# Expert stage of a gated cross-attention and mixture-of-experts block: one TensorE semaphore for each step of a pair, copies and picks in other steps, no clear behind the result scatters

## The chip, the cores and the metric

The kernel runs on one core of a Trainium2 chip. The metric is the device time of one execution in microseconds (us), the median of several runs; less is better. The core has five engines with queues of their own: TensorE (PE in the profile, its weight loads PEld), VectorE (DVE), ScalarE (ACT), GpSimd (POOL) and SyncE (SP). They meet by semaphores alone. Transfers are issued from SP, ACT and POOL and share 16 DMA engines.

## What is computed

The reference, cut to what matters here (x is 4 x 1024 tokens of 256 numbers):

```python
x = x + tanh(g_xattn) * xattn(layernorm(x), ctx_768, mask)
h = layernorm(x)                       # 4096 tokens x 256
topk_idx, topk_w = router(h)           # 6 of 32 experts a token
routed = sum over the token's 6 experts e of  w_e * (relu(h @ up_e.T) ** 2) @ down_e.T    # 256 -> 128 -> 256
shared = (relu(h @ up_s.T) ** 2) @ down_s.T                                               # 256 -> 512 -> 256
x = x + tanh(g_ffn) * (routed + shared)
```

All of it is float32. The 4096 x 6 routed rows are dealt with expert by expert, in tiles of 128 rows that belong to one expert.

## The kernel before

**Stages.** The first stage goes over the 32 token tiles: attention, router, and on POOL the scatter of each normed row to its six places in `routed_rows` in DRAM. The expert stage follows, and it is the one that changes. It has 224 tiles of 128 rows, taken two at a time: `N_PAIRS` = 112 pairs. A short tail adds the last results and stores them.

**A pair p on its way.** SP loads its two row tiles into `ring` (`mid` in the rows), six pairs deep (`load_rows`, L351). PE transposes them into PSUM (`rows_t`, L1337), ACT copies that to `xt` (`save_rows_t`, L581) and copies the two experts' up weights to `w_up` (`copy_up`, L594). PE multiplies (`expert_up`, L1349). DVE squares the positive part into `h_t` (`relu_square`, L977 and L979). PE multiplies with the down weights (`expert_down`, L1364). The result is scaled by the router's weight and goes to `y_sb`, one of eight buffers, by ACT for an even pair (L603) and by DVE for an odd one (L986); both are called `save_out`. POOL scatters `y_sb` to `token_parts` in DRAM, two indirect DMAs a pair (L442). Weights and destinations come from `pick_rows` on DVE (L963 to L972), once for two pairs; SP reloads a place of the ring only after it.

**Steps.** Each engine runs through the same steps p by a loop written out in its own order. On PE a step is `expert_up(p)`, `rows_t(p + 2)`, `expert_down(p - 1)`, and then in 20 steps (`SHARED_STEP`: p = 2, 7, 12 to 97) a piece of the shared expert (L1235 or L1244). PE signals three times in a step: `s_eup`, `s_xtp` and `s_edn`, each with the last matmul of its part. DVE starts on step p's hidden values at `s_eup`, ACT on the rows of pair p + 2 at `s_xtp`, and `save_out` at `s_edn`.

**Adding parts.** Once all pairs of a segment of tokens are scattered, ACT loads six parts of a token tile back (L616) and DVE adds them to `x_all` in three pieces, one a step (L994, L996 and L997, L999). `PART_LOAD` says in which steps. There are 28 such tiles, the first load in step 32; the last four tiles are loaded by SP at the end and summed on PE (L1390).

**The clear.** Behind every scatter POOL runs `pause`: it waits for the clear before, and clears 320 bf16 numbers of a buffer that nobody reads (L413).

```python
            def pause():
                if paused[0]:
                    pool.wait_ge(s_pause, paused[0])
                else:
                    pool.wait_ge(s_xb, NT)
                paused[0] += 1
                nc.gpsimd.memset(bias_o[:].bitcast(BF16)[:, 0:PAUSE], 0.0).then_inc(s_pause, 1)
```

Of the kernel before, what the change touches and what calls it, by code (L numbers as in the profile page):

```python
# [61 lines left out]
DONE = [-(-((TOPK * P * t + NE * (P - 1)) // P) // 2) for t in SEG_END[:-1]]  # L62
PART_LOAD = {DONE[g] + 4 + 3 * i: 4 * g + i for g in range(6) for i in range(4)}
PART_LOAD.update({DONE[6] + 4 + 2 * i: 24 + i for i in range(4)})
STORED = sum(p + 13 < N_PAIRS for p in PART_LOAD)
N_EARLY, N_LAST = len(PART_LOAD), NT - SEG_END[6]
SHARED_STEP = {2 + 5 * i: i for i in range(8 * (NBLK - GAP) - TB)}


def flamingo_block(nc, x, ctx_t, mask, g_xattn, g_ffn, w_q, w_k, w_v, w_o, b_o, gate_t, e_bias,  # L70
# [7 lines left out]
    with ExitStack() as ctx:  # L78
# [189 lines left out]
        s_ld = [sem(f"rows_loaded_{i}") for i in range(6)]  # L268
        s_xtp = sem("rows_t_psum")
        s_xts = sem("rows_t")  # L270
        s_eup = sem("expert_hidden_psum")
        s_ewu = sem("expert_up_weights_copied")
        s_eht = sem("expert_hidden_t")
        s_edn = sem("expert_out_psum")
        s_ey = [sem(f"expert_out_by_{e}") for e in ("act", "dve")]
# [34 lines left out]
        def _(sp):  # L310
# [32 lines left out]
            def load_rows(p):  # L343
                if p % 2 == 0:
                    sp.load(regs[p // 2 % 4], row_i[0:1, 2 * p:2 * p + 4])
                if p >= 6:
                    sp.wait_ge(s_xtp, p - 5)
                    sp.wait_ge(s_pick, (p - 6) // 2 + 1)
                for j in range(2):
                    at = sp.snap(regs[p // 2 % 4][p % 2 * 2 + j], min_val=0, max_val=DUMMY + NE * P)  # L350
                    sp.dma_start(ring[:, p % 6, j, :], rows[bass.ds(at, P), :]).then_inc(s_ld[p % 6], 16)  # L351
# [9 lines left out]

            sp.wait_ge(s_edn, N_PAIRS)
            for i in range(N_LAST):
# [11 lines left out]
        def _(pool):  # L375
# [63 lines left out]
            for p in range(N_PAIRS):  # L439
                pool.wait_ge(s_ey[p % 2], p // 2 + 1)  # L440
                for j in range(2):
                    nc.gpsimd.indirect_dma_start(  # L442
                        parts, bass.IndirectOffsetOnAxis(ap=place[:, p // 2 % 8, p % 2 * 2 + j:p % 2 * 2 + j + 1], axis=0),
                        y_sb[p % 8][:, j * D:(j + 1) * D], None,
                        bounds_check=bound, oob_is_err=False).then_inc(s_ys[p % 8], 16)
                    pause()

        @block.scalar
        def _(act):
# [129 lines left out]
            def save_rows_t(p):  # L579
                act.wait_ge(s_xtp, p + 1)  # L580
                A.activation(xt[:, p % 2, :], ps[:, p % 2, :], ACT.Copy).then_inc(s_xts, 1)  # L581
# [15 lines left out]
            def save_out(p):  # L597
                act.wait_ge(s_edn, p + 1)
                act.wait_ge(s_pick, p // 2 + 1)
# [18 lines left out]
            for p in range(2):  # L618
                save_rows_t(p)
                copy_up(p)  # L620
            for p in range(N_PAIRS + 1):
                if p + 2 < N_PAIRS:
                    save_rows_t(p + 2)
                    copy_up(p + 2)
                if p % 2:
                    save_out(p - 1)
                if p in SHARED_STEP and SHARED_STEP[p] % 8 < 4:
# [8 lines left out]
        def _(dve):  # L636
# [337 lines left out]
            def relu_square(p):  # L974
                dve.wait_ge(s_eup, p + 1)
                h, r = ps[:, 2 + p % 2, 0:256], relu[p % 2]
# [4 lines left out]
            def save_out(p):  # L981
                dve.wait_ge(s_edn, p + 1)
                if p >= 8:
# [16 lines left out]

            pick_rows(0)
            for p in range(N_PAIRS + 1):
# [12 lines left out]
            for p, t in PART_LOAD.items():  # L1015
                for step in range(3):
                    if p + 3 + step > N_PAIRS:
                        add_parts(t, step)
                        dve.drain()
# [14 lines left out]
        def _(pe):  # L1034
# [296 lines left out]
            def rows_t(p):  # L1331
# [7 lines left out]
                ins.then_inc(s_xtp, 1)  # L1339

# [3 lines left out]
            def expert_up(p):  # L1344
                pe.wait_ge(s_xts, p + 1)
                pe.wait_ge(s_ewu, p + 1)
                for j in range(2):
                    for c in range(KC):
                        ins = M(ps[:, 2 + p % 2, j * P:(j + 1) * P], w_up[p % 2][:, j, c * P:(c + 1) * P],  # L1349
                                xt[:, p % 2, j * 256 + c * P:j * 256 + (c + 1) * P],  # L1350
                                start=c == 0, stop=c == KC - 1, skip_group_check=True)
                ins.then_inc(s_eup, 1)

            def expert_down(p):
# [3 lines left out]
                if p < 2:  # L1358
                    pe.wait_ge(s_acc, 2 * GAP - 1 + p)
                elif p % 2 == 0:  # L1360
                    pe.wait_ge(s_ey[0], p // 2)
                for j in range(2):
# [3 lines left out]
                            start=True, stop=True, skip_group_check=True)  # L1366
                ins.then_inc(s_edn, 1)

            rows_t(0)
            rows_t(1)  # L1370
            for p in range(N_PAIRS + 1):
# [86 lines left out]
```

## Time and profile before

| | |
|---|---|
| median of 3 runs | 860.59 us (860.07 to 863.73) |
| the profiled execution's own time | 863.49 us |
| its span, from first to last instruction | 861.3 us |
| expert stage: first and last start of `expert_up` | 488.3 and 831.1 us |
| busy: PE, POOL, DVE, ACT | 87%, 76%, 61%, 48% of the span |
| granted TensorE clock, mean | 0.958 |

The expert stage runs from 488 us to some 835 us, 40% of the span; what stands before it is not touched by the change. A busy PE is not PE at its peak, since matmuls are pipelined and their ends are modelled. The rows below give start and length of single instructions in the stage, and sums over stretches of it.

### The profile page before, as it was taken

What the parts mean: (1) busy time and instruction counts of PE and PEld (TensorE: products, weight loads), DVE (VectorE), ACT (ScalarE), POOL (GpSimd) and SP (SyncE); (2) the same over time, 40 slices, a digit from 0 to 9 for tenths busy, and PEclk for the clock granted to TensorE, in tenths of its full rate; (3) what the DMA queues carried; (4) which work ended last, traced back from release to release, by engine and by line L of the source; (5) the groups of instructions that cost most, each with busy time, mean ns of one, the idle gap of its engine ahead of it and who ended that gap; (6) DMA issues with size and microseconds to landing.
All of it is one profiled execution on the core that took longest, in us unless ns stands there. A gap on an engine that the chain in (4) does not pass through costs nothing.

```text
span 861.3 us, 17905 instructions
## 1 busy us (share of the span) xinstructions
PE 746.5 (87%) x5420; PEld 620.5 (72%) x5420; DVE 522.1 (61%) x1744; ACT 415.8 (48%) x1251; POOL 651.4 (76%) x903
## 2 busy tenths in 40 slices
PE   5889998998889898879899498879989699897877
PEld 4778886877768787756548387768877588686765
DVE  0765485866757676765632144555776577686773
ACT  1366655555535555535222265555555545565530
POOL 1254346597969898888888388888898889898883
PEclk9999999899989999999989699999999999999998
DMA  9900001231212212426373455557888789798845
GB/s 303 307 2 2 2 2 67 79 139 67 81 67 74 87 74 87 164 86 250 126 268 134 139 172 168 177 165 227 282 263 288 250 260 283 236 314 267 250 142 178
DMA packets 77663, 140.55 MB, mean 163 GB/s; under 512 B 13686, under 2 KB 60033, under 8 KB 77056
## 3 DMA queue, kind: packets, MB, share of 16 engines
q1 hardware_dynamic: 50896, 63.26, 24.1%
q0 software_dynamic: 19968, 52.34, 16.4%
q10 hardware_dynamic: 6704, 23.80, 9.1%
q8 instruction: 45, 0.74, 0.3%
q14 instruction: 50, 0.41, 0.2%
HBM read 73.80 MB, written 69.73 MB: 167 GB/s over the span
## 4 chain that ended last, share of the span: by engine, by line
PE 54%; POOL 14%; DVE 10%; another core or an unknown queue 6%; issue 5%; ACT 5%; DVEq 3%; DMA 2%; ACTq 1%; SPq 0%; POOLq 0%
PE ps L1364 10%; PE ps L1349 10%; POOL routed_rows L419 10%; PE ps L1152 5%; PE ps L1162 5%; PE ps L1337 4%; PE ps L1103 4%; POOL bias_o L413 4%; PE ps L1053 4%; PE ps L1140 3%; PE ps L1244 2%; PE ps L1235 2%; ACT att L498 2%; DMA picked<-in_mask 1%
## 5 line engine op out<-in xcount | busy, mean ns | idle before, releaser
L413 POOL MEMSET bias_o<- 128x320 bf16 x416 | 163.8, 394 | 0.1
L1364 PE MATMUL ps<-big,att 128*128 x448 | 123.3, 398 | 39.8 <-DVE att L979 23.8
L581 ACT ACTIVATE att<-ps 128x512 f32<-128x512 f32 x112 | 66.8, 596 | 164.0 <-PE ps L1337 104.5
L419 POOL DMA_INDIRECT routed_rows<-x_n,slots x120 | 124.4, 1036 | 25.2 <-issue 19.7
L442 POOL DMA_INDIRECT token_parts<-hid,place x112 | 113.1, 1010 | 36.4 <-issue 17.4
L1349 PEld LDWEIGHTS ps<-att 128*128 128x128 f32 x896 | 118.3, 196 | 22.1 <-issue 17.8
L1349 PE MATMUL ps<-att 128*128 128x128 f32 x896 | 123.2, 282 | 4.4 <-issue 2.7
L1364 PEld LDWEIGHTS ps<-big,att 128*128 128x128 f32 x448 | 77.5, 193 | 59.0 <-issue 52.2
L507 ACT ACTIVATE att<-ps 128x512 f32<-128x512 f32 (+1 forms) x96 | 47.5, 540 | 80.1 <-PE ps L1140 52.5
L1337 PE MATMUL ps<-cst,mid 128*128 128x128 f32 x448 | 70.1, 281 | 13.1 <-DMA mid<-routed_rows 13.1
L594 ACT ACTIVATE att<-big 128x256 f32 x224 | 80.3, 410 | 2.0 <-issue 1.6
L1152 PE MATMUL ps<-att,big 128*64 128x128 f32 x1024 | 69.4, 281 | 8.9 <-DVE x_all L720 4.1
L402 POOL TENSOR_TENSOR att<-att,rsum 128x1232 f32<-128x1232 f32 x14 | 31.4, 2245 | 57.0 <-DVE rsum L711 57.0
L1152 PEld LDWEIGHTS ps<-att,big 128*64 128x64 f32 x1024 | 58.6, 139 | 17.5 <-issue 6.3
L1162 PE MATMUL ps<-hid,big 128*128 128x256 f32 x256 | 67.0, 408 | 1.7 <-issue 1.5
L498 ACT ACTIVATE att<-ps,nmax 128x154 f32<-128x154 f32 x176 | 65.7, 408 | 5.6 <-DVE nmax L706 5.6
L1103 PE MATMUL ps<-big 64*128 64x154 f32 x512 | 52.4, 320 | 18.1 <-remote 15.0
L1337 PEld LDWEIGHTS ps<-cst,mid 128*128 128x128 f32 x448 | 54.8, 146 | 13.9 <-issue 13.5
L1053 PEld LDWEIGHTS ps<-x1t,hid 128*128 128x128 f32 x512 | 63.1, 195 | 2.1 <-issue 0.5
L706 DVE TENSOR_REDUCE nmax<-ps 128x3 f32<-128x462 f32 (+1 forms) x96 | 49.9, 572 | 24.1 <-PE ps L1103 23.3
L1053 PE MATMUL ps<-x1t,hid 128*128 128x128 f32 x512 | 63.5, 278 | 0.0
L1103 PEld LDWEIGHTS ps<-big 64*128 64x128 f32 x512 | 45.7, 197 | 24.1 <-remote 16.6
(239 smaller groups left out, 1472.7 us busy)
## 6 DMA issues: line engine op xcount, KB each, us to landing
mid<-routed_rows SPq DMA_DIRECT2D x224, 138.0 KB
big<-token_parts ACTq DMA_DIRECT2D x19, 768.0 KB
x_n<-token_parts ACTq DMA_DIRECT2D x9, 768.0 KB
routed_rows<-pad_row SPq DMA_DIRECT2D x1, 4416.0 KB
routed_rows<-pad_row SPq DMA_DIRECT2D x32, 138.0 KB
big<-in_x SPq DMA_DIRECT2D x4, 1024.0 KB, 17.5
big<-in_w_moe SPq DMA_DIRECT2D x2, 2048.0 KB, 8.7
big<-in_w_moe SPq DMA_DIRECT2D x1, 4096.0 KB
```

The lines of the kernel that those rows point to most:

```text
L413: nc.gpsimd.memset(bias_o[:].bitcast(BF16)[:, 0:PAUSE], 0.0).then_inc(s_pause, 1)
L419: nc.gpsimd.indirect_dma_start(rows, bass.IndirectOffsetOnAxis(ap=slots[:, t, k:k + 1], axis=0), normed(t), None).then_inc(s_sca[t // TB % ...
L442: nc.gpsimd.indirect_dma_start(parts, bass.IndirectOffsetOnAxis(ap=place[:, p // 2 % 8, p % 2 * 2 + j:p % 2 * 2 + j + 1], axis=0), y_sb[p ...
L498: ins = A.activation(prob[T % 3][:, h * JP:h * JP + J], ps[:, q, i * J:(i + 1) * J], ACT.Exp, bias=nmax[:, T % 2, h:h + 1], accum_out=esum ...
L594: ins = A.activation(w_up[p % 2][:, j, :], w_exp[:, bass.ds(e, 1), 0:256].rearrange("p a n -> p (a n)"), ACT.Copy)
L1053: ins = M(ps[:, 6, m * P:(m + 1) * P], wq[:, c, m * P:(m + 1) * P], x1t[:, c, :], start=c == 0, stop=c == KC - 1, skip_group_check=True)
L1103: return M(ps[:, q, at:at + J], q_t[r, m, :], k_all[r, m, b * J:(b + 1) * J], start=False, stop=True, skip_group_check=True)
L1152: ins = M(ps[h % 2 * DH:(h % 2 + 1) * DH, 7, h // 2 * P:(h // 2 + 1) * P], v_all[b][:, at:at + DH], prob_t[:, c * P:(c + 1) * P], start=c ...
L1162: ins = M(ps[:, 7, 0:D], att_t[:, m * P:(m + 1) * P], wo[:, m, :], start=m == 0, stop=m == MC - 1, skip_group_check=True)
L1337: ins = nc.tensor.transpose(ps[:, p % 2, j * 256 + c * P:j * 256 + (c + 1) * P], ring[:, p % 6, j, c * P:(c + 1) * P], ident)
L1349: ins = M(ps[:, 2 + p % 2, j * P:(j + 1) * P], w_up[p % 2][:, j, c * P:(c + 1) * P], xt[:, p % 2, j * 256 + c * P:j * 256 + (c + 1) * P], ...
L1364: ins = M(ps[:, 6 + p % 2, j * D:(j + 1) * D], h_t[:, p % 2, j * P:(j + 1) * P], w_exp[:, bass.ds(e, 1), 256:512].rearrange("p a n -> p (a ...
```

## The change

Four things are changed in the expert stage.

1. PE signals once in a step, `s_step`, with the last instruction of the step's three parts; `ROWS_T`, `UP` and `DOWN` = 1, 3, 5 are the counts at which the rows, the hidden values and the results of pair 0 stand.
2. PE's step p becomes `expert_down(p - 2)`, `expert_up(p)`, `rows_t(p + 2)`. `expert_down` of an odd pair now waits for DVE's `save_out` by name.
3. `save_out(p - 2)` runs in step p, on ACT in even steps and on DVE in odd ones (before: `save_out(p - 1)`, ACT in odd steps, DVE in even ones). `pick_rows(q)` runs in step 2q, behind `relu_square(2q)` (before: step 2q - 1). The parts are loaded and added one step later. The loops have one step more.
4. The `pause` behind the result scatters is gone; behind the row scatters of the first stage it stays.

```diff
-PART_LOAD = {DONE[g] + 4 + 3 * i: 4 * g + i for g in range(6) for i in range(4)}
+PART_LOAD = {DONE[g] + 5 + 3 * i: 4 * g + i for g in range(6) for i in range(4)}
...
+ROWS_T, UP, DOWN = 1, 3, 5
...
                 if p >= 6:
-                    sp.wait_ge(s_xtp, p - 5)
+                    sp.wait_ge(s_step, ROWS_T + p - 6)
                     sp.wait_ge(s_pick, (p - 6) // 2 + 1)
...
                         bounds_check=bound, oob_is_err=False).then_inc(s_ys[p % 8], 16)
-                    pause()
...
             def save_rows_t(p):
-                act.wait_ge(s_xtp, p + 1)
+                act.wait_ge(s_step, ROWS_T + p)
...
             def save_out(p):
-                act.wait_ge(s_edn, p + 1)
+                act.wait_ge(s_step, DOWN + p)
...
-                if p % 2:
-                    save_out(p - 1)
+                if p >= 2 and p % 2 == 0:
+                    save_out(p - 2)
...
             def relu_square(p):
-                dve.wait_ge(s_eup, p + 1)
+                dve.wait_ge(s_step, UP + p)
...
-                if p >= 2 and p % 2 == 0:
-                    save_out(p - 1)
-                if p % 2 and p + 1 < N_PAIRS:
-                    pick_rows((p + 1) // 2)
+                if p >= 3 and p % 2:
+                    save_out(p - 2)
+                if p % 2 == 0 and p < N_PAIRS:
+                    pick_rows(p // 2)
...
-                elif p % 2 == 0:
-                    pe.wait_ge(s_ey[0], p // 2)
+                else:
+                    pe.wait_ge(s_ey[p % 2], p // 2)
...
-            for p in range(N_PAIRS + 1):
+            for p in range(N_PAIRS + 2):
+                if p >= 2:
+                    last = expert_down(p - 2)
                 if p < N_PAIRS:
-                    expert_up(p)
+                    last = expert_up(p)
                 if p + 2 < N_PAIRS:
-                    rows_t(p + 2)
-                if p >= 1:
-                    expert_down(p - 1)
+                    last = rows_t(p + 2)
+                last.then_inc(s_step, 1)
```

On PE, in the middle of the expert stage, two steps stood like this before (ISA and TENSOR_LOAD are register work for the expert's number):

```order
L1349 MATMUL ps<-att 128x128 [waits expert_up_weights_copied,rows_t]
L1349 MATMUL ps<-att 128x128 x3
L1337 MATMUL ps<-cst,mid 128x128 [waits rows_loaded_2]
L1337 MATMUL ps<-cst,mid 128x128 x3
L1342 ISA [waits expert_hidden_t]
L1364 MATMUL ps<-big,att 128x256
L1342 ISA
L1364 MATMUL ps<-big,att 128x256
L1244 MATMUL ps<-w_shared,hid 128x256 [waits late_shared_added]
L1244 MATMUL ps<-w_shared,hid 128x256 x3
```

The same place on PE with the change:

```order
L1346 MATMUL ps<-att 128x128 [waits expert_up_weights_copied,rows_t]
L1346 MATMUL ps<-att 128x128 x3
L1334 MATMUL ps<-cst,mid 128x128 [waits rows_loaded_2]
L1334 MATMUL ps<-cst,mid 128x128 x3
L1241 MATMUL ps<-w_shared,hid 128x256 [waits late_shared_added]
L1241 MATMUL ps<-w_shared,hid 128x256 x3
L1339 ISA [waits expert_out_by_dve,expert_hidden_t]
L1361 MATMUL ps<-big,att 128x256
```

The down matmuls have moved from the end of a step to the start of the next, behind the shared piece, and those of an odd pair wait for DVE's `save_out` too.

On DVE the two steps of an even and an odd pair stood like this before (`hot` and `x_n` are the relu buffers of an even and an odd pair):

```order
L977 TENSOR_SCALAR hot<-ps 128x256 [waits expert_hidden_psum]
L979 SCALAR_TENSOR_TENSOR att<-ps,hot 128x256
L986 TENSOR_TENSOR hid<-ps,pair_w 128x512 [waits expert_out_scattered_1,expert_out_psum]
L977 TENSOR_SCALAR x_n<-ps 128x256 [waits expert_hidden_psum]
L979 SCALAR_TENSOR_TENSOR att<-ps,x_n 128x256
L963 TENSOR_TENSOR is_e<-mid,tile_key 128x24 [waits rows_loaded_3,expert_out_scattered_5,expert_out_scattered_4,rows_loaded_2]
```

And with the change:

```order
L975 TENSOR_SCALAR x_n<-ps 128x256 [waits expert_steps_done]
L977 SCALAR_TENSOR_TENSOR att<-ps,x_n 128x256
L984 TENSOR_TENSOR hid<-ps,pair_w 128x512 [waits expert_out_scattered_1,expert_steps_done]
L975 TENSOR_SCALAR hot<-ps 128x256 [waits expert_steps_done]
L977 SCALAR_TENSOR_TENSOR att<-ps,hot 128x256
L961 TENSOR_TENSOR is_e<-mid,tile_key 128x24 [waits rows_loaded_3,expert_out_scattered_5,expert_out_scattered_4,rows_loaded_2]
```

`save_out` has gone from behind the relu of an even pair to behind that of an odd one, the picks the other way, and all of them hang on the one count of steps.

On POOL the last two scatters stood so before, the clears between and behind them:

```order
L442 DMA token_parts<-big,place 53248x256 [waits expert_out_by_dve]
L413 MEMSET bias_o 128x320 [waits scatter_paused]
L442 DMA token_parts<-big,place 53248x256
L413 MEMSET bias_o 128x320 [waits scatter_paused]
```

And with the change:

```order
L441 DMA token_parts<-big,place 53248x256 [waits expert_out_by_dve]
L441 DMA token_parts<-big,place 53248x256
```

Nothing stands between the two scatters of a pair any more.

## Rows read from the trace of the kernel before

**Rows 1.** Sums by stretch of the expert stage, without and with parts to add.

```profile
core 0: us, PE busy (x) PEld busy (x) DVE busy (x) ACT busy (x) POOL busy (x), PEclk, DMA share, GB/s
488.00:588.00 100.00, 88.95 (x556) 77.30 (x557) 50.66 (x163) 57.34 (x141) 81.30 (x119) 0.97 0.57 170
588.00:831.00 243.00, 212.90 (x1331) 180.84 (x1330) 169.82 (x495) 131.85 (x328) 215.26 (x310) 0.99 0.82 261
...
600.00:650.00 50.00, 45.72 (x287) 38.52 (x286) 38.16 (x110) 29.07 (x73) 44.73 (x64) 1.00 0.88 278
```

**Rows 2.** Single lines: `expert_up`'s matmuls, and ACT's loads of parts.

```profile
L1349 PE MATMUL ps<-att x896: 272/275/550, 488.3 to 831.1; 128*128 128x128 f32 x180
...
L616 ACTq DMA_DIRECT2D big<-token_parts x19: 326/326/336, 588.8 to 830.4; - x19
```

**Rows 3.** Waits from 500 to 830 us: us in total, times, longest.

```profile
ACT att L581 <- PE ps L1337: 79.0, 46, 3.4
ACT att L581 <- remote: 54.2, 33, 3.9
...
PE ps L1364 <- DVE att L979: 20.9, 24, 2.8
```

**Rows 4.** Timeline while POOL scatters: start, length, then idle time before.

```profile
622.43 1.13 PE L1349 MATMUL ps<-att 128*128 128x128 f32 x8
...
623.39 0.60 PE L1337 MATMUL ps<-cst,mid 128*128 128x128 f32 x4
...
624.24 0.99 POOL L442 DMA_INDIRECT token_parts<-hid,place  x1 [0.17 <-issue]
...
624.89 0.42 DVE L977 TENSOR_SCALAR hot<-ps 128x256 f32<-128x256 f32 x1 [2.29 <-PE ps L1349]
...
625.20 0.41 POOL L413 MEMSET bias_o<- 128x320 bf16 x1
...
625.67 0.60 ACT L581 ACTIVATE att<-ps 128x512 f32<-128x512 f32 x1 [2.66 <-remote]
...
625.77 0.99 POOL L442 DMA_INDIRECT token_parts<-hid,place  x1 [0.17 <-issue]
...
625.97 0.48 PE L1364 MATMUL ps<-big,att 128*128 x1 [1.98 <-DVE att L979]
```

**Rows 5.** Timeline before the first result scatter.

```profile
492.58 0.60 ACT L581 ACTIVATE att<-ps 128x512 f32<-128x512 f32 x1 [0.15 <-PE ps L1337]
...
493.25 1.05 PE L1349 MATMUL ps<-att 128*128 128x128 f32 x8
...
493.69 0.83 ACT L603 ACTIVATE hid<-ps,pair_w 128x256 f32<-128x256 f32 x2
...
494.14 0.60 PE L1337 MATMUL ps<-cst,mid 128*128 128x128 f32 x4
...
494.34 0.42 DVE L977 TENSOR_SCALAR hot<-ps 128x256 f32<-128x256 f32 x1 [0.30 <-PE ps L1349]
...
494.79 1.00 POOL L442 DMA_INDIRECT token_parts<-hid,place  x1 [14.22 <-ACT hid L603]
...
494.84 0.42 DVE L979 SCALAR_TENSOR_TENSOR att<-ps,hot 128x256 f32<-128x256 f32 x1
```

**Rows 6.** Timeline: two steps of PE in a row without a stall.

```profile
607.21 1.05 PE L1349 MATMUL ps<-att 128*128 128x128 f32 x8
...
609.40 1.05 PE L1349 MATMUL ps<-att 128*128 128x128 f32 x8
```

**Rows 7.** The chain that ended last, a shared piece: start, us, what.

```profile
603.45 1.73 PE ps L1244 x8
```

**Rows 8.** Groups, 500 to 830 us: busy, mean ns, idle before.

```profile
L986 DVE TENSOR_TENSOR hid<-ps,pair_w 128x512 f32<-128x512 f32 x27 | 18.5, 687 | 12.8 <-PE ps L1364 7.4 <-remote 4.4 <-issue 1.0
...
L1337 PE MATMUL ps<-cst,mid 128*128 128x128 f32 x424 | 65.0, 277 | 0.0
...
L442 POOL DMA_INDIRECT token_parts<-hid,place x107 | 108.1, 1011 | 21.5 <-issue 16.7 <-DVE hid L986 4.2 <-ACT hid L603 0.4
```

More of the change, by code:

```diff
@@ L62 @@
 DONE = [-(-((TOPK * P * t + NE * (P - 1)) // P) // 2) for t in SEG_END[:-1]]
-PART_LOAD = {DONE[g] + 4 + 3 * i: 4 * g + i for g in range(6) for i in range(4)}
-PART_LOAD.update({DONE[6] + 4 + 2 * i: 24 + i for i in range(4)})
+PART_LOAD = {DONE[g] + 5 + 3 * i: 4 * g + i for g in range(6) for i in range(4)}
+PART_LOAD.update({DONE[6] + 5 + 2 * i: 24 + i for i in range(4)})
 STORED = sum(p + 13 < N_PAIRS for p in PART_LOAD)
 N_EARLY, N_LAST = len(PART_LOAD), NT - SEG_END[6]
+ROWS_T, UP, DOWN = 1, 3, 5
 SHARED_STEP = {2 + 5 * i: i for i in range(8 * (NBLK - GAP) - TB)}
@@ L268, in flamingo_block @@
         s_ld = [sem(f"rows_loaded_{i}") for i in range(6)]
-        s_xtp = sem("rows_t_psum")
+        s_step = sem("expert_steps_done")
         s_xts = sem("rows_t")
-        s_eup = sem("expert_hidden_psum")
         s_ewu = sem("expert_up_weights_copied")
         s_eht = sem("expert_hidden_t")
-        s_edn = sem("expert_out_psum")
         s_ey = [sem(f"expert_out_by_{e}") for e in ("act", "dve")]
@@ L360, in _ @@
                     store(PART_LOAD[p - 13])
-            sp.wait_ge(s_edn, N_PAIRS)
+            sp.wait_ge(s_step, DOWN + N_PAIRS - 1)
             for i in range(N_LAST):
@@ L981, in save_out @@
             def save_out(p):
-                dve.wait_ge(s_edn, p + 1)
+                dve.wait_ge(s_step, DOWN + p)
                 if p >= 8:
@@ L999, in add_parts @@
                     V.tensor_tensor(x_all[:, t, :], x_all[:, t, :], g[:, 0, :], ALU.add).then_inc(s_fin, 1)
-            pick_rows(0)
-            for p in range(N_PAIRS + 1):
+            for p in range(N_PAIRS + 2):
                 if p < N_PAIRS:
                     relu_square(p)
-                if p >= 2 and p % 2 == 0:
-                    save_out(p - 1)
-                if p % 2 and p + 1 < N_PAIRS:
-                    pick_rows((p + 1) // 2)
+                if p >= 3 and p % 2:
+                    save_out(p - 2)
+                if p % 2 == 0 and p < N_PAIRS:
+                    pick_rows(p // 2)
                 if p in SHARED_STEP and SHARED_STEP[p] % 8 >= 4:
@@ L1016, in _ @@
                 for step in range(3):
-                    if p + 3 + step > N_PAIRS:
+                    if p + 3 + step > N_PAIRS + 1:
                         add_parts(t, step)
@@ L1338, in rows_t @@
                                                   ring[:, p % 6, j, c * P:(c + 1) * P], ident)
-                ins.then_inc(s_xtp, 1)
+                return ins
             def expert(p, j):
@@ L1351, in expert_up @@
                                 start=c == 0, stop=c == KC - 1, skip_group_check=True)
-                ins.then_inc(s_eup, 1)
+                return ins
             def expert_down(p):
@@ L1366, in expert_down @@
                             start=True, stop=True, skip_group_check=True)
[L1367 to L1371, printed above, removed]
+                return ins
+            rows_t(0).then_inc(s_step, 1)
+            rows_t(1).then_inc(s_step, 1)
+            for p in range(N_PAIRS + 2):
+                if p >= 2:
+                    last = expert_down(p - 2)
                 if p < N_PAIRS:
-                    expert_up(p)
+                    last = expert_up(p)
                 if p + 2 < N_PAIRS:
-                    rows_t(p + 2)
-                if p >= 1:
-                    expert_down(p - 1)
+                    last = rows_t(p + 2)
+                last.then_inc(s_step, 1)
                 if p in SHARED_STEP:
```

## The prediction

> **What bounds the kernel now.** I read the sums by stretch first, then the waits, then the timeline; the reader is to see that no engine is short of time in the expert stage, and that TensorE's signals come late.
>
> The stage has 112 steps. `expert_up` starts at 488.3 us and its last matmul at 831.1 [rows 2], so 111 steps take 342.8 us, 3.09 us each. The first load of parts, in step 32, is at 588.8 us [rows 2]: 33 steps take 100.5 us (3.05 each), and the 78 behind them, with parts to add, take 242.3 us (3.11 each). Where PE is not held up, a step is 2.19 us (607.21 to 609.40) [rows 6], and a shared piece adds 1.73 us [rows 7] in 20 of the steps. Free of stalls PE would need 2.19 + 7 x 1.73 / 33 = 2.56 us a step in the first part and 2.19 + 13 x 1.73 / 78 = 2.48 in the second. So 0.5 to 0.6 us a step are lost. VectorE is busy for 169.82 us of the second part, 2.2 us a step; with some 0.25 us between its instructions (0.08 inside a relu, 494.34 to 494.84 [rows 5]) it needs 2.4 [rows 1]. ACT needs less [rows 1]. POOL is busy for 215.26 of 243 us [rows 1], and with the 0.17 us of issue before a scatter, 1.53 us each (624.24 to 625.77 [rows 4]), 3.06 us a pair: all of its time, though it is waited for by nobody in the waits.
>
> The waits name who waits: ACT for the rows in PSUM, 79.0 us and, where the view finds no releaser, 54.2; PE for the relu, 20.9 [rows 3]. The timeline says why. Before the first result scatter `expert_up` ends at 493.25 + 1.05 = 494.30 and the relu starts at 494.34; `rows_t` ends at 494.74 [rows 5]. At 622 us, with POOL scattering, `expert_up` ends at 623.56 and an idle VectorE starts at 624.89, 1.33 us late; `rows_t` ends at 623.99, an idle ACT starts at 625.67, 1.68 us late, and PE stands idle for 1.98 us until its down matmuls can start [rows 4]. The late starts come just behind marks of POOL: 0.65 us into the scatter of 624.24, and 0.06 us behind the end of the clear (625.20 + 0.41). The second signal did not pass with the first, though both were due. I read it so: while POOL issues scatters, a TensorE signal passes only twice in 1.53 us, often one at a time. Three in a step, 3.2 in the mean with those of the shared pieces, need 3.2 x 0.76 = 2.4 us at that rate, more than PE's own 2.19. That is the bound.
>
> **The change, part by part.**
>
> *One signal a step.* It takes two of three signals away, 336 - 116 = 220 in all. None can queue behind another of the same step. What is left is the wait for the next place.
>
> *Its price.* The relu now starts behind `rows_t` too, 0.44 us later than `expert_up`'s end (494.30 to 494.74 [rows 5]). The down matmuls of p come at the start of step p + 2, so the relu has step p + 1 for itself, 2.19 us, and needs 0.92 (494.34 to 494.84 + 0.42 [rows 5]): 1.27 to spare. `save_out` on VectorE ends 0.92 + 0.69 [rows 8] = 1.61 behind the signal, 0.58 to spare. On ACT it is tighter: copy of rows, two weight copies and `save_out` take from 492.58 to 493.69 + 0.83 = 1.94 us [rows 5], and the down matmuls two pairs on start 2.19 us behind the signal; before, nearly a whole step more was left. 0.25 us to spare, unless step p + 1 has a shared piece. Queued behind such a waiting down matmul are PE's `expert_up` and `rows_t`, and behind the signal all of VectorE's and ACT's step.
>
> *No clear.* No row shows two scatters without a clear between. I take 0.98 us and the 0.17 of issue, 1.15 each and 2.3 a pair, from the scatters' own rows (0.99 single, 1.01 in the mean) [rows 4, 8]; at best 0.98, at worst 1.53 as now, if something else fills the gap. POOL then has time left, 0.5 us a step at 2.8. The place behind the clear is gone; the one 0.65 us into a scatter stays, so one in 1.15 us. A signal waits 0 to 1.15 us, 0.58 in the mean, during 2.3 of 2.8 us: I take 0.5. The bounds are 0 (a free place behind each scatter) and the whole of a pair's scatters, 2.13 us.
>
> *What that costs.* On ACT's way a wait spread over 0 to 1.15 us exceeds 0.25 by 0.35 us in the mean, times 0.82 for POOL's share, every second step, less the fifth with a shared piece: 0.35 x 0.82 x 0.5 x 0.8 = 0.12 us a step. The other ways keep their slack.
>
> *Picks one step later.* SP's reload waits for the pick, so it is later by a step, 2.8 us, with six pairs of room; today PE never waits for rows here (0.0 us idle [rows 8]). I cost it at nothing; if the cover goes, it would be at most the 2.8 us once in two steps. Parts move with the step that precedes them, and nothing waits for them now.
>
> *Sum.* First part: 2.56 + 0.12 + 0.07 for the clock (0.97 granted [rows 1]) = 2.75, 33 steps are 90.8 us, 9.7 less. Second part: 2.48 + 0.12 + 0.02 for the clock (0.99), and 0.2 by my choice, because VectorE (2.4) is near and the DMA engines, busy for 0.82 at 3.11 us a step [rows 1], come to 0.90: 2.82, 78 steps are 220.0 us, 22.3 less. Start and tail: nothing, though POOL ends nearer to PE. 32.0 us less than the profiled 863.5 gives 831.5; that execution was 2.9 us over the median, so 829.
>
> *A rule against it.* The Trainium skill, TensorE: Matmul & The Clock Gate, Why this matters for your kernels, prices a semaphore increment at about 26 ns. By that 220 fewer would save at most 5.7 us, some 855 by estimate. The rows show 1.33 and 1.68 us instead of it.
>
> **The rivals.**
>
> *Both engines come to their floor* (0.16). If a place is free behind each scatter, steps are 2.6 and 2.6: 33 x 0.45 + 78 x 0.51 = 55 us less, 806; the middle of this case is 811. For it: the summed slack above. Against it: the DMA share would be 0.98, over the 0.88 that is the highest of a 50 us stretch [rows 1].
>
> *The signals were not the bound* (0.08): the stalls belong to the order on VectorE and ACT, and the tighter `save_out` gives back what is won, 856 to 864. For it: much of the idle time is before `relu` and the rows' copy, which PE feeds. Against it: the 1.3 to 1.7 us with an idle reader.
>
> *Back-to-back scatters shut TensorE's signals out* (0.15), the case on the other side. POOL starts a pair when `save_out` is done, 1.61 or 1.94 us behind a signal; PE's next step ends at 2.19, that is 0.25 to 0.58 us into the first scatter, time and again. If the clear was what let signals by, each waits to the pair's end, 1.55 to 1.88 us, mean 1.7. ACT's way then loses 0.4 x (1.7 - 0.25) = 0.58 a step, the relu's 0.4 x (1.7 - 1.27) = 0.17 (0.4 being half the steps, less those with a shared piece): 3.26 and the clock make 3.3, 111 x 0.21 = 23 us more, 884. It decides at a mean lateness of 1.45 us. For it: a place just behind the clear in [rows 4]. Against it: the other place lies inside a scatter.
>
> **How the numbers follow.** My forecast (815 to 848) has 0.50, between it and no change (848 to 856) 0.09, no change 0.08, slower 0.15, the floor case (under 815) 0.16, and 0.02 is left. 0.5% (4.3 us) is about what a measurement of this kernel can tell from no change. Faster: 0.50 + 0.16 + 0.09 and some of the rest, 0.77; same 0.08; slower 0.15. The range is 807 to 862: below it lies a third of the floor case, above it the slower case.
>
> **What would show it.** Right: `expert_up`'s starts 2.8 us apart, from 488 to some 800 us; scatters of a pair 1.15 us apart and POOL idle between pairs; ACT's and VectorE's idle time before L579 and L975 short, their starts within 0.7 us of `rows_t`'s end; DMA share near 0.9. Wrong: starts of both readers at the end of a pair's scatters, 1.5 us and more behind `rows_t` (slower case); PE idle before the down matmuls with ACT's `save_out` as releaser for more than 0.3 us every second step; PE idle before L1334, which would be rows that come late; or a scatter that grows well over 0.98 us.

## The result

The changed kernel is slower: median 903.97 us (889.55 to 1812.09, 4 runs) against 861.51 (860.07 to 863.73), a ratio of 1.038 [1.032, 1.044]. The ratio goes by the two executions of 889.55 and 898.06 us (mean 893.8); those of 909.89 and 1812.09 us are slow ones, and are left out of it. The profile is of the one of 909.89 us (span 907.8), 16 us above that mean, so its loss is larger than the ratio's; nothing below rests on that of 1812.09.

A first warning on that number: on other chips the same kernel is 5% faster than the one before.

`expert_up` by its source line, and three groups of the page, after the change (engine, operation, names, count; duration min/median/max in ns, first and last start in us; for the groups busy us, mean ns, idle before them):

```profile
L1346 PE MATMUL ps<-att x896: 272/275/552, 490.9 to 874.0; 128*128 128x128 f32 x180
```

```profile
L1361 PE MATMUL ps<-big,att 128*128 x448 | 130.5, 417 | 75.2 <-DVE hid L984 20.9
L441 POOL DMA_INDIRECT token_parts<-hid,place x112 | 115.1, 1028 | 93.7 <-ACT hid L601 38.6
L579 ACT ACTIVATE att<-ps 128x512 f32<-128x512 f32 x112 | 66.7, 596 | 211.7 <-PE ps L1334 133.6
```

The stage starts 2.6 us later than in [rows 2], and takes 383.1 us where it took 342.8: a step is 3.45 us, not 3.09. With 3.6 us more behind the last `expert_up` (33.8 against 30.2) these are the 46.5 us by which the two spans differ. The loss is thus in the steps. Sums by stretch have the columns of [rows 1]:

```profile
500.00:600.00 100.00, 81.37 (x495) 70.79 (x494) 43.30 (x145) 48.69 (x123) 56.35 (x58) 0.95 0.50 151
600.00:700.00 100.00, 80.35 (x487) 69.12 (x487) 59.89 (x177) 49.38 (x123) 58.07 (x57) 0.96 0.72 232
```

POOL, busy for 81 and 89% in [rows 1], is busy for 56 and 58%; PE has fallen from 89 and 88% to 81 and 80%, DVE and ACT fell too, and the DMA share to 0.50 and 0.72. Nobody is short of time. (The granted clock fell as well, to 0.94 over the stage from 0.98, and PE's busy time there rose from 302 to 314 us; that is 12 of the 40 us, the rest is PE standing idle.) The waits from 480 to 880 us (us in total, times, longest):

```profile
ACT att L579 <- PE ps L1334: 133.6, 53, 22.4
...
POOL token_parts L441 <- ACT hid L601: 38.6, 10, 17.8
...
POOL token_parts L441 <- DVE hid L984: 24.4, 12, 3.2
```

The 22.4 and the 17.8 us are the start of the stage. Without them ACT still waits for the rows more than in [rows 3], and now POOL waits for results, which it hardly did before [rows 8]. The timeline of two steps shows what they wait for (start, length, engine and what; in brackets idle time and releaser):

```profile
641.92 0.60 ACT L579 ACTIVATE att<-ps 128x512 f32<-128x512 f32 x1 [1.15 <-PE ps L1334]
...
642.38 0.60 PE L1334 MATMUL ps<-cst,mid 128*128 128x128 f32 x4
...
645.01 0.99 POOL L441 DMA_INDIRECT token_parts<-hid,place  x1 [0.30 <-issue]
...
645.56 0.60 PE L1334 MATMUL ps<-cst,mid 128*128 128x128 f32 x4
647.09 0.60 ACT L579 ACTIVATE att<-ps 128x512 f32<-128x512 f32 x1 [3.96 <-PE ps L1334]
647.09 0.42 DVE L975 TENSOR_SCALAR hot<-ps 128x256 f32<-128x256 f32 x1 [2.91 <-PE ps L1334]
...
648.91 0.60 ACT L579 ACTIVATE att<-ps 128x512 f32<-128x512 f32 x1
...
649.29 1.12 PE L1361 MATMUL ps<-big,att 128*128 x4 [3.12 <-ACT hid L601]
649.30 0.98 POOL L441 DMA_INDIRECT token_parts<-hid,place  x1 [3.31 <-ACT hid L601]
```

A step's one signal is due when `rows_t` ends: here at 642.98 and at 646.16. ACT copies the rows once a step, in order, so the signals and the copies can be counted off against each other: the copy at 647.09 answers the signal of 642.98, and the one at 648.91 that of 646.16. ACT and DVE, both idle, thus start together 4.1 us late, 2.08 us behind the start of the last of three scatters, with POOL idle since 646.00. The trace has two updates of the semaphore there, at 647.07 and 647.23: the signal of 646.16 passed right behind the older one, 1.07 us late. PE and POOL then both stand until ACT's `save_out` is done.

**How often signals are late, and by how much.** The trace also records when a semaphore is updated, though some of the records are missing. Set against the end of the last matmul before it that carries an update, this gives a share used below ("late"): of TensorE's updates in the expert stage, those over 0.1 us behind. It is 76% before (of 287 recorded) and 75% after.

That is how often; for how much it is no measure, since a signal that comes behind the next one's matmul is held against the wrong end. How much comes from counting in order, signal by reader, where the reader stood idle. After, the first reader of a signal starts 1.4 us late in the mean (82 signals; over 2 us for 24 of them, 4.3 at most); over all 110, idle reader or not, it is 1.5. Before, `relu_square` starts 2.2 us behind its `expert_up` in the mean (67 idle starts; 4.6 at most). Where signals are prompt, as in f1 below, the same count gives 0.04 us for every idle reader. So the changed kernel's signals are, in the mean, no later than those of before, and it is slower all the same.

### The profile page after: what moved, and what is told of

Its sections match the earlier page's. It is cut to its first block, busy times and chain, and to the rows that moved or that the text cites. A ratio compares the mean times of both kernels' runs of the same rounds, so it can differ in the third digit from the quotient of the medians.

```text
span 907.8 us, 17736 instructions
## 1 busy us (share of the span) xinstructions
PE 758.1 (84%) x5420; PEld 638.4 (70%) x5420; DVE 521.6 (57%) x1744; ACT 413.3 (46%) x1251; POOL 571.7 (63%) x679
## 4 chain that ended last, share of the span: by engine, by line
PE 52%; POOL 13%; DVE 10%; issue 7%; another core or an unknown queue 6%; DVEq 5%; ACT 3%; DMA 2%; ACTq 1%; SPq 0%; POOLq 0%
PE ps L1361 9%; POOL routed_rows L418 9%; PE ps L1346 9%; PE ps L1334 6%; PE ps L1159 5%; PE ps L1149 4%; PE ps L1100 4%; PE ps L1050 4%; POOL bias_o L412 3%; PE ps L1137 3%; PE ps L1241 2%; DVEq L1011 2%; PE ps L1232 1%; DMA picked<-in_mask 1%
## 5 line engine op out<-in xcount | busy, mean ns | idle before, releaser
L1361 PE MATMUL ps<-big,att 128*128 x448 | 130.5, 417 | 75.2 <-DVE hid L984 20.9
L1361 PEld LDWEIGHTS ps<-big,att 128*128 128x128 f32 x448 | 83.0, 203 | 101.9 <-issue 94.4
L1346 PEld LDWEIGHTS ps<-att 128*128 128x128 f32 x896 | 128.7, 208 | 8.1 <-issue 1.1
L1346 PE MATMUL ps<-att 128*128 128x128 f32 x896 | 129.0, 291 | 0.7 <-ACT att L592 0.7
L1334 PE MATMUL ps<-cst,mid 128*128 128x128 f32 x448 | 71.8, 286 | 12.4 <-DMA mid<-routed_rows 12.4
L412 POOL MEMSET bias_o<- 128x320 bf16 x192 | 73.4, 383 | 0.1
L975 DVE TENSOR_SCALAR hot<-ps 128x256 f32<-128x256 f32 x56 | 23.7, 424 | 85.9 <-PE ps L1334 57.1
L1159 PE MATMUL ps<-hid,big 128*128 128x256 f32 x256 | 70.5, 424 | 2.1 <-issue 1.9
L1149 PE MATMUL ps<-att,big 128*64 128x128 f32 x1024 | 65.0, 276 | 4.9 <-DVE x_all L718 2.7
L975 DVE TENSOR_SCALAR x_n<-ps 128x256 f32<-128x256 f32 x56 | 23.7, 424 | 73.9 <-PE ps L1334 43.2
L1334 PEld LDWEIGHTS ps<-cst,mid 128*128 128x128 f32 x448 | 57.0, 150 | 13.0 <-issue 12.8
L1149 PEld LDWEIGHTS ps<-att,big 128*64 128x64 f32 x1024 | 56.1, 137 | 12.0 <-issue 5.7
## 6 DMA issues: line engine op xcount, KB each, us to landing
big<-token_parts ACTq DMA_DIRECT2D x19, 768.0 KB
x_n<-token_parts ACTq DMA_DIRECT2D x9, 768.0 KB
```

Of the source, the lines that this page charges most:

```text
L1149: ins = M(ps[h % 2 * DH:(h % 2 + 1) * DH, 7, h // 2 * P:(h // 2 + 1) * P], v_all[b][:, at:at + DH], prob_t[:, c * P:(c + 1) * P], start=c ...
L1159: ins = M(ps[:, 7, 0:D], att_t[:, m * P:(m + 1) * P], wo[:, m, :], start=m == 0, stop=m == MC - 1, skip_group_check=True)
L1361: ins = M(ps[:, 6 + p % 2, j * D:(j + 1) * D], h_t[:, p % 2, j * P:(j + 1) * P], w_exp[:, bass.ds(e, 1), 256:512].rearrange("p a n -> p (a ...
```

## The experiments

Kernels of one set ran on one chip, beside the kernel before. "Pace" is the first to the last step's start of `expert_up`, over 111.

| set, chip, before's median | run | ratio [95%] | `expert_up` steps | pace | late |
|---|---|---|---|---|---|
| 1, chip 10, 861.11 | e1: new order, clear kept | 1.010 [1.005, 1.014] | 487.9 to 828.6 | 3.07 | 72% |
| | e2: old order, no clear | 1.037 [1.027, 1.046] | 483.8 to 861.2 | 3.40 | 62% |
| | e3: new order, clear of 32 | 1.057 [1.047, 1.067] | 491.0 to 875.9 | 3.47 | 64% |
| | e4: old order, one signal | 1.000 [0.994, 1.007] | 488.2 to 825.6 | 3.04 | 68% |
| 2, chip 13, 844.18 | e5: clear between two | 0.973 [0.969, 0.976] | 470.8 to 784.3 | 2.82 | 0% |
| | e6: clear behind a pair | 0.972 [0.968, 0.976] | 470.7 to 781.5 | 2.80 | 0% |
| | e7: plain stores | 0.965 [0.962, 0.968] | 476.6 to 783.8 | 2.77 | 0% |
| | e8: old order, clear of 256 | 0.990 [0.985, 0.994] | 472.2 to 796.7 | 2.92 | 0% |
| 3, chip 3, 844.01 | f1: changed kernel | 0.952 [0.948, 0.956] | 473.7 to 771.9 | 2.69 | 0% |
| | f2: as e6 | 0.969 [0.965, 0.972] | 474.0 to 785.7 | 2.81 | 0% |
| | f3: as e7 | 0.963 [0.959, 0.967] | 472.1 to 778.4 | 2.76 | 0% |
| | f4: as e1 | 1.000 [0.999, 1.002] | 474.4 to 808.4 | 3.01 | 0% |
| 4, chip 15, 863.93 | g1: as e7 | 0.967 [0.958, 0.975] | 488.2 to 797.6 | 2.79 | 0% |
| | g2: as e6 | 1.043 [1.035, 1.050] | 497.0 to 867.6 | 3.34 | 68% |
| 5, chip 6, 844.33 | h1: as e5 | 0.973 [0.969, 0.976] | 473.2 to 786.3 | 2.82 | 0% |
| | h2: as e8 | 0.989 [0.985, 0.992] | 475.7 to 798.9 | 2.91 | 0% |
| | h3: changed kernel | 0.950 [0.944, 0.956] | 471.6 to 768.0 | 2.67 | 0% |
| 6, chip 8, 864.66 | k1: as e5 | 1.030 [1.021, 1.040] | 484.3 to 846.9 | 3.27 | 71% |

The sets fall into two kinds. On chips 10, 15 and 8, and on that of the first result, the kernel before takes 861 to 865 us and signals are late ("late chips"); on chips 13, 3 and 6 it takes 844 and no signal is late in any kernel profiled there ("prompt chips").

### Set 1: one part of the change at a time

e1 puts the clear back into the changed kernel:

```diff
                         bounds_check=bound, oob_is_err=False).then_inc(s_ys[p % 8], 16)
+                    pause()
```

> The changed kernel with the clear of 320 numbers put back behind every result scatter (the last part of the change undone, the rest kept). Theory A (the clear lets TensorE's signals by; without it they wait some 2 us behind the start of a scatter): the loss of the change is gone, but POOL needs 3.06 us a pair again, so 850 to 862 us. Theory B (the loss is from the new order: save_out one step tighter on ACT, relu behind rows_t): 885 us or more, as the changed kernel.

Measured 1.010: nearly all of the loss is gone. That POOL sets the pace is seen on POOL's timeline:

```profile
640.34 0.99 POOL L441 DMA_INDIRECT token_parts<-picked,place  x1 [0.17 <-issue]
641.30 0.41 POOL L412 MEMSET bias_o<- 128x320 bf16 x1
641.87 0.99 POOL L441 DMA_INDIRECT token_parts<-x_n,place  x1 [0.16 <-issue]
```

It scatters every 1.53 us without a gap, 3.06 a pair, and the pace is 3.07, though 72% of the signals are late. The remaining 1% is POOL's as well, by its trace: the new order begins to scatter 2.2 us later (497.0 against 494.8 us in the profile of before) and ends at 851.4 against 846.8, and the chain that ended last is scatters and clears up to that end, then the last tiles' parts:

```profile
848.84 0.99 POOL token_parts L441
849.83 0.38 POOL bias_o L412
850.21 0.04 issue
850.25 0.12 POOLq L79
850.38 2.54 DMA token_parts<-big,place
```

e2 takes the clear alone out of the kernel before (`-pause()` at the same place).

> The kernel before with only the clear behind the result scatters taken away; three signals a step and the old order. Theory A: three signals a step wait for scatters to land, so slower than before and at least as slow as the changed kernel, 890 to 930 us. Theory B: POOL is merely faster, which nobody waits for, 855 to 862 us.

Measured 1.037, the same as the whole change, at a pace of 3.40. With e1 this shows that on this chip the loss is that of the missing clear.

e3 keeps a clear, but a short one, of 32 numbers:

```diff
-            def pause():
+            def pause(n=PAUSE):
...
-                nc.gpsimd.memset(bias_o[:].bitcast(BF16)[:, 0:PAUSE], 0.0).then_inc(s_pause, 1)
+                nc.gpsimd.memset(bias_o[:].bitcast(BF16)[:, 0:n], 0.0).then_inc(s_pause, 1)
...
                         bounds_check=bound, oob_is_err=False).then_inc(s_ys[p % 8], 16)
+                    pause(32)
```

> The changed kernel with a clear of 32 numbers in place of 320 behind every result scatter. Theory A1 (it is the clear's event that lets a signal by, whatever its length): signals pass once per scatter, POOL needs some 2.5 us a pair, 825 to 845 us. Theory A2 (it is the time between scatters that matters): little better than the changed kernel, 870 to 890 us. Theory B: 885 us or more.

Measured 1.057, worse than no clear in the old order (e2), and above both figures of theory A. The group of the clear from 500 to 860 us:

```profile
L412 POOL MEMSET bias_o<- 128x32 bf16 x206 | 32.7, 159 | 0.0
```

It takes 0.16 us and hides in the time between two scatters, which stay 1.29 us apart. That an instruction of another kind stands between scatters does not help; that every scatter stays 1.53 us from the next does.

e4 leaves order and clears as before, and signals once in a step:

```diff
+ROWS_T, UP, DOWN = 1, 3, 4
...
                 if p < N_PAIRS:
-                    expert_up(p)
+                    last = expert_up(p)
                 if p + 2 < N_PAIRS:
-                    rows_t(p + 2)
+                    last = rows_t(p + 2)
                 if p >= 1:
-                    expert_down(p - 1)
+                    last = expert_down(p - 1)
+                last.then_inc(s_step, 1)
```

> The kernel before with one TensorE signal a step, at the end of its old order of up, rows, down, and the clear kept. Theory A: fewer signals to let by, but POOL's 3.06 us a pair stays, 850 to 860 us. Theory B: the relu waits for rows and down matmuls too, 862 to 880 us.

Measured 1.000 [0.994, 1.007]: 220 signals fewer bring nothing while the clear is there. The prediction's main gain is refuted on the kind of chip on which signals are late.

### Sets 2 and 3: other spacings, and no scatters at all

e5 clears only between the two scatters of a pair (`if j == 0: pause()` in the changed kernel), e6 only behind the pair (`pause()` behind the loop over `j`). e7 has no result scatters; SP stores the same bytes to rows in order, so the parts of a token are not where the reference wants them:

```diff
-            for p in range(N_PAIRS):
+            for p in range(N_PAIRS + 8):
...
+                if p >= 8:
+                    r = p - 8
+                    sp.wait_ge(s_ey[r % 2], r // 2 + 1)
+                    for j in range(2):
+                        sp.dma_start(parts[(2 * r + j) * P:(2 * r + j + 1) * P, :],
+                                     y_sb[r % 8][:, j * D:(j + 1) * D]).then_inc(s_ys[r % 8], 16)
```

e8 is the kernel before with a clear of 256 numbers instead of 320 (`pause(256)`).

> The changed kernel with the clear of 320 numbers only between the two scatters of a pair, none behind the second. Theory A (TensorE's signals pass at the end of a long clear or when a scatter has landed, some 2.1 us behind its start): a signal due in the second scatter waits to its landing, so most of the loss stays, 875 to 895 us. Theory C (one passing place a pair is enough, since there is one signal a step): 845 to 862 us.

> The changed kernel with the clear of 320 numbers only behind the second scatter of a pair. Theory A: signals pass once a pair, at the clear's end, 0.7 us earlier than at the landing: 865 to 885 us. Theory C: 845 to 862 us.

> The changed kernel, its result scatters replaced by plain stores of the same tiles, issued by SP to rows that follow each other, so that the results are not put at their tokens' places; POOL is idle in the stage, the bytes moved are the same. Theory A (POOL's scatters hold up TensorE's signals): signals come within 0.1 us, steps of 2.6 to 2.8 us, 810 to 840 us. Theory B or a bound by the DMA engines: 860 us or more, signals still late.

> The kernel before with a clear of 256 numbers in place of 320 behind the result scatters. By the durations of 32 and 320 numbers it should take some 0.33 us and end some 1.31 us behind the scatter's start, a scatter each 1.47 us in place of 1.53. If the clear only has to end behind the scatter's own 1.29 us, signals still pass there and the time is 845 to 860 us; if 320 is the least that works, 875 us or more.

All four are faster than before, by 2.7, 2.8, 3.5 and 1.0%, and no signal is late in any of them. e5, e6 and e8 came out below every figure expected of them. As this chip had no late signal to begin with, set 2 says nothing on what spacing lets signals by. It does say that something else bounds the kernel here. Set 3 ran the two kernels that had contradicted each other, the changed one and e1, on one chip, with e6 and e7 again.

> The changed kernel itself, once more. The four runs before this one were all on a chip where TensorE's signals came on time beside the scatters (the last four profiles), where the first ones were not. Theory A (late signals make the loss, and whether they are late depends on the chip): on a chip with late signals 1.03 to 1.05 of before; on one with prompt signals 0.96 to 0.98. Theory D (the lost clear costs by itself, for instance by scatters that crowd other transfers): 1.02 or more on any chip.

> The changed kernel with all clears back, once more. POOL needs 3.06 us a pair and begins a step later, so 1.00 to 1.01 of before where signals are late; where they are prompt before is POOL-bound too, so the same 1.00 to 1.01.

> The changed kernel with the clear of 320 numbers behind the second scatter of each pair only, once more. Theory A: about 0.97 of before where signals are prompt, as then; where they are late, between the changed kernel and the one with all clears, 1.00 to 1.03. Theory D: 0.97 anywhere.

> The changed kernel with plain stores from SP in place of the scatters (results not at their tokens' places), once more. Theory A: no late signal on any chip, as POOL issues nothing, 0.94 to 0.97 of before. If TensorE's signals are late here too on a chip where they are late with scatters, POOL's scatters are not what holds them: 1.0 or more.

f1, the changed kernel itself, takes 804.21 us against 844.01, 39.8 us less. `expert_up` by its line, and the sums of the same two stretches as above:

```profile
L1346 PE MATMUL ps<-att x896: 272/275/552, 473.7 to 772.6; 128*128 128x128 f32 x180
```

```profile
500.00:600.00 100.00, 96.26 (x638) 85.97 (x637) 64.09 (x200) 61.41 (x154) 72.87 (x74) 1.00 0.74 230
600.00:700.00 100.00, 97.60 (x636) 86.10 (x635) 80.62 (x241) 63.89 (x157) 75.78 (x74) 1.00 0.95 313
```

PE is at 96 and 98% with a granted clock of 1.00, and the DMA share reaches 0.95 without a loss of pace (2.67 in the first 33 steps, 2.69 in the rest). Its timeline, at a place like that of the slow profile:

```profile
645.24 0.98 POOL L441 DMA_INDIRECT token_parts<-hid,place  x1 [0.30 <-issue]
...
646.53 0.98 POOL L441 DMA_INDIRECT token_parts<-hot,place  x1 [0.30 <-issue]
...
646.71 0.60 PE L1334 MATMUL ps<-cst,mid 128*128 128x128 f32 x4
...
647.34 0.60 ACT L579 ACTIVATE att<-ps 128x512 f32<-128x512 f32 x1 [1.95 <-PE ps L1334]
647.34 0.42 DVE L975 TENSOR_SCALAR x_n<-ps 128x256 f32<-128x256 f32 x1 [0.89 <-PE ps L1334]
...
647.82 0.98 POOL L441 DMA_INDIRECT token_parts<-hot,place  x1 [0.30 <-issue]
```

`rows_t` ends at 647.31 in the middle of a scatter, and both readers start at 647.34, 0.03 us later: the same program, a signal due while POOL scatters, and no delay. Three scatters start 1.29 us apart, all of POOL's time.

f4 is 1.000 [0.999, 1.002]. Order and single signal are in it, the clear is too: on a prompt chip they bring nothing while the clear is there, and all of f1's gain, 844.77 to 804.21 us, comes from taking it away. POOL's scatters of f4 from 500 to 780 us, their idle time and who waited for them:

```profile
  issue: 29.5, 179
...
  ACT att L580: 21.8, 4
```

POOL was idle for no reason but its own issue. And the pace of every kernel on a prompt chip follows POOL's cycle for a pair, from 0.98 us a scatter, 0.17 of issue, 0.41 for a full clear, and 0.30 between two bare scatters:

| kernel | POOL's pair | pace |
|---|---|---|
| f4, clear behind each | 2 x 1.53 = 3.06 | 3.01 |
| e8, h2, clear of 256 | 2 x 1.47 = 2.94 | 2.92, 2.91 |
| e5, h1, e6, f2, one clear a pair | 1.53 + 1.29 = 2.82 | 2.82, 2.82, 2.80, 2.81 |
| f1, h3, no clear | 2 x 1.29 = 2.58 | 2.69, 2.67 |

The pace may be a little below the cycle, since eight buffers let POOL run behind: in f4 the last scatter starts at 831.7 us, 22.5 us behind the last `expert_up`. For f1 the floor of 2.58 is not quite met: scatters with nothing but issue between them start 1.32 us apart in the mean, 2.64 a pair, since some take longer than 0.98 us, and POOL is idle for some 10 us beyond issue. POOL is not far ahead of the others there: e7, f3 and g1 (below), without any scatter, are no faster (2.77, 2.76, 2.79), and PE's weight loads wait for row tiles from DRAM there, 17.6 us in g1. What bounds those is not shown.

### Sets 4, 5 and 6: the two kinds of chips again

> Plain stores from SP in place of the scatters, to be seen on a chip with late signals (before at about 861 us). Theory A: POOL's scatters are what holds TensorE's signals, so with POOL idle none is late in the expert stage and the time is 0.95 to 0.97 of before there too, while the row scatters of the first stage keep some late. Theory E (such a chip's signals are late whatever POOL does, once transfers are many): late in the expert stage as well, 1.00 or more. On a chip with prompt signals (before at about 844 us) 0.96 to 0.97 again, which tells nothing new.

> One clear of 320 numbers a pair, behind its second scatter, to be seen on a chip with late signals. Theory A: signals pass once a pair behind the clear and seldom else, so between the changed kernel and the one with all clears, 1.01 to 1.03 of before. On a chip with prompt signals 0.97 again.

Chip 15 was a late one. g2, the same kernel as e6 and f2 (0.97), is 1.043 here, with 68% late: over the 1.01 to 1.03 expected, and no better than the changed kernel. g1 has no result scatters, and no late signal in the expert stage, though 28% are late in its first stage (100 to 330 us), where POOL still scatters rows. Its sums and a piece of its timeline:

```profile
500.00:780.00 280.00, 267.50 (x1733) 233.94 (x1731) 200.42 (x609) 174.42 (x429) 0.00 (x0) 1.00 0.88 272
```

```profile
651.31 0.66 PE L1333 MATMUL ps<-cst,mid 128*128 128x128 f32 x4
...
652.00 0.60 ACT L578 ACTIVATE att<-ps 128x512 f32<-128x512 f32 x1 [1.61 <-PE ps L1333]
652.01 0.42 DVE L974 TENSOR_SCALAR hot<-ps 128x256 f32<-128x256 f32 x1 [0.53 <-PE ps L1333]
```

Readers start 0.03 us behind `rows_t`, with the DMA engines busy for 0.88. On a late chip, then, it is POOL's indirect scatters that hold TensorE's signals up, not the load on the DMA engines; the pace, 2.79, is that of e7 and f3 on prompt chips.

> The clear of 320 numbers only between the two scatters of a pair, to be seen on a chip with late signals. If a place between two scatters is what lets signals by, 1.00 to 1.02 of before and signals that pass at the clear's end; if every scatter needs one, about 1.04 as with the clear behind the pair. On a chip with prompt signals 0.97 again.

> The kernel before with clears of 256 numbers, to be seen on a chip with late signals. A clear that ends behind the scatter's own 1.29 us lets signals by: 0.98 to 1.00 of before. If 320 is near the least that works: 1.03 or more. On a chip with prompt signals 0.99 again.

> The changed kernel once more. On a chip with late signals (before at about 861 us) 1.03 to 1.05 of before; on one with prompt signals (before at about 844 us) 0.95.

> The clear of 320 numbers only between the two scatters of a pair, once more, to be seen on a chip with late signals: 1.00 to 1.02 of before if the place between two scatters is what lets signals by, about 1.04 if every scatter needs its clear. On a chip with prompt signals 0.97 again, which tells nothing new.

Chip 6 was prompt: h1, h2 and h3 repeat e5, e8 and f1 within 0.2% of the ratio. The question of h1 and h2, how a thinner clear does where signals are late, was left to k1. On chip 8, a late one, one clear a pair gives 1.030 and 71% late: better than none (1.038) by less than the intervals tell apart, worse than one behind every scatter (1.010 for e1).

## Why the prediction was wrong

The forecast of 829 us came out at 904 on the first chip, at 804 and 800 on two others. By its own steps:

**"That is the bound"** failed. The late signals were there, and later than it read, but with a clear behind every scatter they did not set the pace. POOL did, at 3.06 us a pair. The text had that very figure and put it aside because POOL was "waited for by nobody in the waits". POOL may run up to eight buffers behind, and then whoever needs a free one waits for a scatter; f4's view shows 21.8 us of such waiting in four pieces, [rows 3] none that I took for it. The right reading of [rows 8] was the other side: of POOL's 21.5 us of idle time 16.7 are its issue, so it hardly waited. e4 (1.000), f4 (1.000) and the pace of e1 (3.07) show it.

The lateness itself was read against the wrong matmuls. The down matmuls of 625.97 in [rows 4] are those of the pair before the `expert_up` of 622.43, and they waited for the relu of 624.89. So that relu, and the copy of 625.67, answer the step before, whose parts stood in the trace of before at:

```profile
620.12 1.05 PE L1349 MATMUL ps<-att 128*128 128x128 f32 x8
...
621.01 0.60 PE L1337 MATMUL ps<-cst,mid 128*128 128x128 f32 x4
```

The relu starts 3.72 us behind its signal and the copy 4.06, not 1.33 and 1.68. What does hold is the two places: of the late updates of before, 90 come 0.6 to 0.9 us behind the start of the last scatter, 131 come 1.3 to 1.6 us behind it, none elsewhere.

**"One signal a step"**: worth nothing on either kind of chip with the clear kept (e4, f4); without the clear, on a late chip, three signals a step in the old order (e2, 1.037) do as well as one in the new (1.038, on another chip).

**"Its price"**, slacks of 0.25 to 1.27 us: hardly charged where signals are prompt (f1's PE is idle before its down matmuls for 7.1 us in all); on the late chip it is 75.2 us, 0.67 a step where 0.12 was forecast (39.8 us in all in the profile of before). The new order costs 1% in e1, where POOL starts later and ends later. "Picks one step later" cost nothing: PE's idle time before L1334 is 12.4 us in the whole profile after, at loads from DRAM.

**"No clear"** is the step that turned the sign. It took the place "0.65 us into a scatter" for the scatter's own, and so one place in 1.15 us and a mean lateness of 0.5. Without clears, signals due during scatters pass mostly 1.6 to 2.4 us behind the start of the last one, some at 0.7 to 1.1; the mean lateness, counted in order, is 1.4 to 1.5 us, three times the chosen 0.5 and below the bound of 2.13, and single signals, at up to 4.3 us, are beyond it. Bare scatters are 1.29 us apart, not 1.15: 0.30 us lie between, not 0.17.

**The rival that won** is the third, back-to-back scatters shutting the signals out, at 0.15: 3.3 us a step and 884 us, against 3.45 and 904. It stands in the trace as described, both readers at one moment far behind `rows_t`, PE waiting for ACT's `save_out`. Its sum went by the mean, with waits of 1.55 to 1.88 us, and called 1.45 us no loss; measured were 1.4 to 1.5 us and a step 0.36 us longer. The waits spread over 0 to 4.3 us, and a signal can miss more than one pair of scatters. My reading, argued only: with one signal for rows, hidden values and results, a late one delays all three users at once, and none of them works ahead. Mean lateness alone does not explain the loss: in e2 the relu starts 1.9 us behind its signal in the mean (44 idle starts), no later than the 2.2 of before, and a step is 0.32 us longer. The Trainium skill's rule (TensorE: Matmul & The Clock Gate, Why this matters for your kernels), some 26 ns for an increment, fits the 0.03 us of f1 and g1, and not the 4.1 and 1.07 us of the profile after: it is borne out here where no scatter holds a signal up.

**The right value for a wrong reason.** On prompt chips the change gains 39.8 and 43.9 us where 32.0 were forecast; f1's steps are 2.67 us in the first part and 2.69 in the second (forecast 2.75 and 2.82). That is luck as far as the mechanism goes: the cause is POOL's shorter cycle and not the signals. Of the 0.2 us for VectorE and the DMA engines no sign is seen: the DMA share went to 0.95, and the pace of the second part is 0.02 above that of the first.

**What the change is.** One edit decides it, the missing clear. Where signals are prompt, it takes 0.48 us from POOL's pair and gives 5%. Where they are late, it brings scatters so near to each other that signals pass mostly when POOL has run dry: PE waits for `save_out`, POOL for PE, and 4% are lost. Best on prompt chips is the changed kernel, on late ones the kernel before; no version tried with scatters beats both.

**Open.** Why a clear of 320 behind every scatter lets enough signals by, and one a pair, or 32 numbers, does not; and why signals no later in the mean cost more without it. e8's 256 was never run on a late chip. Whether the new order and the single signal are needed for the 5%: the old order without the clear was never run on a prompt chip. What path a signal shares with a scatter's issue: no run shows it. Whether the kind belongs to the chip or to what surrounds it at the time: each chip was met once. That it explains the 17 to 21 us between before's medians is argued only: of the kernels profiled, the stage before the expert stage ends at 484 to 497 us on late chips, 471 to 477 on prompt ones (with 28 to 38% of its signals late on late chips), and that is most of it.

## What to carry to other kernels

Hold a late start against its own signal, by counting both in order, and not against the nearest end. An engine that nobody waits for can be the bound if it drains a ring of buffers: look at whether it is ever idle for want of input, and compare its cycle with the pace. Before a pause or a dummy operation is removed, ask what passes during it, and try its removal alone; before signals are merged, check that the engines behind them can work ahead by the lateness that the trace shows. And a gain or loss of some per cent that hangs on signal latency is to be measured on more than one chip.

## What the hardware showed that I had not expected

- One program has two times on chips of one kind: before's median was 861 to 865 us on four chips and 844 on three; the changed kernel gave 904, 804 and 800 us.
- On the slower kind 62 to 76% of TensorE's semaphore updates come over 0.1 us late while POOL issues indirect scatters, and single ones wait over 4 us; with plain stores by SP, of the same bytes, none.
- Two bare indirect scatters of 128 rows are 1.29 us apart: 0.98 busy and 0.30 between; a clear of 32 numbers (0.16 us) fits in between for nothing.
- A scatter stretches beside some VectorE work: from 0.98 to 1.45 us in f1, when an addition of 128x768 runs. The 40 scatters of f1 that overlap one take 1.12 us in the mean, the 184 others 0.99:

```profile
648.78 0.95 DVE L992 TENSOR_TENSOR big<-big 128x768 f32<-128x768 f32 x1
...
649.14 1.45 POOL L441 DMA_INDIRECT token_parts<-picked,place  x1 [0.34 <-DVE picked L984]
```
